# One reciprocal for the sums of a row's first two tiles, and GpSimd's weighing of both moved into the second turn

## The chip, the cores and the metric

The kernel runs on one core of a Trainium2 chip. The metric is device time in microseconds (us): the time of one execution, as a median over runs. The core has five engines that work side by side and hand work over by semaphores: TensorE (PE, matrix products into PSUM), VectorE (DVE), ScalarE (ACT), GpSimd (POOL) and SyncE (SP, DMA issues here). Each engine works its own list of instructions strictly in order, so an instruction that waits holds up all that stand behind it on its engine.

## The reference, cut to what matters

The input is `x` of shape (8, 512, 128). Each of the 8 batch rows has 4 tiles of 128 tokens, 32 tiles in all.

```python
xn = layernorm(x)
s  = attention(xn)                     # windows, compressed blocks and selected tokens, gated, normalised
# product-key expert layer, for each token and each of 8 heads
sx, ix = top_k(sim[0], 16)             # sim: 8 heads x 2 sides x 32 keys
sy, iy = top_k(sim[1], 16)
scores, pk = top_k(sx[:, None] + sy[None, :], 16)
h = gelu(x . W_down[pk]) * softmax(scores)
f = sum(h * W_up[pk])
out = x + s * silu(f)
```

The change touches only the `softmax(scores)`: its denominators are sums over the candidates of a head, inverted and multiplied onto the exponentials.

## The kernel before, in words

Only 50 of the 256 rank pairs of a head can be among its 16 best, so the kernel keeps 8 heads x 50 candidates for each token and finds which are in. A tile n passes these stations, spread over several turns of the loop:

- PE `scores(n)` writes the similarities into `sim_bank[n % 2]`. DVE `first_8` (16 MAX8), `strike_8` (pairs of MATCH_VALUE_LOAD and MATCH_REPLACE8) and `next_8` (16 MAX8) find the 16 best on each side.
- PE `top_columns` transposes them, ACT `take_topT` copies, PE `pair_gaps` makes the candidates' gaps in `t_bank`, ACT `take_gaps` copies them to `gap`. DVE `gaps_of_pairs`, `gaps_of_thirds` and `last_gaps` find a bound, `last8`.
- POOL `past_of`, ACT `side_of`, PE `transpose_sides`, ACT `take_sides`, POOL `square_of`, PE `count_places`, ACT `out_by_of`, POOL `drop_of` turn the bound into what each candidate loses.
- ACT `exps(n)` takes the exponentials into `prob[n % 2]` and, by its accumulator, their 8 sums into `den` (lines 797 to 810).
- DVE `invert_sums(n)` inverts the 8 sums (line 1104, `rden`). POOL `weigh(n)` multiplies (line 499, `wgt`), `add_halves(n)` and `add_quarters(n)` add heads (lines 505 and 512, `wgt4`, `wgt2`). PE `expert_weights(n)` transposes the result into `c_bank` (line 1504). Four tiles on, ACT `weights_out` copies the bank, POOL `gelu_times_weights` multiplies with the GELU values, PE `experts_out` makes the output, ACT `silu_parts` and POOL `gate_silu` gate it (lines 524, 853 to 856, 579).

Each engine has a hand-written function `turn(n)` for n = 4 to 31. With b, j = divmod(n, 4), b is the batch row and j = 0 to 3 the place in it, called here the first to the fourth turn of a row. In a turn n DVE finds the best of tile n, makes the bound of tile n - 1, and inverts the sums of tile n - 4, right behind `first_8(n)`. POOL makes `past` of tile n - 2, `drop` of n - 3, and weighs n - 4. The attention of row b - 1 or b is laid around it, differently in each of the four turns: `maxima` and `inverse_row_sums` (DVE, first turn), `scale_probs` (POOL, first turn), `attention_scores` (PE, first turn), `attention_out` (PE, third turn, in two halves around `top_columns`), `norm2` (POOL, third turn).

Two waits set the place of the vector work. `strike_8(n, 3)` waits until the last MAX8 of `first_8(n)` has signalled (line 1123). `gaps_of_pairs` waits for ACT's `gap` (line 1139).

## Time and profile before

| | us |
|---|---|
| median of three runs | 292.26 |
| the three runs | 293.19, 292.26, 290.89 |
| the profiled execution's own time | 290.93 |
| its span, first to last instruction | 289.2 |
| DVE busy | 267.4 (92%) |
| PE busy | 239.5 (83%) |
| ACT busy | 238.5 (82%) |
| POOL busy | 228.7 (79%) |

Busy is time in which an engine executes. In a row of the trace, an idle time in brackets is how long the engine waited ahead of that instruction, and the arrow names whose result ended the wait. Turns 4 to 31 fill the stretch from 60.4 us to 265 us; what stands before loads and folds weights, what stands behind is the end of the last row.

### The profile page before, as it was taken

To read this page: it belongs to the slowest core of one execution; us is meant where nothing else is said; L and a number is where in the kernel's file an instruction comes from. 1 tells how busy PE (TensorE), PEld (TensorE's weight loads), DVE (VectorE), ACT (ScalarE), POOL (GpSimd) and SP (SyncE) were. 2 spreads that over 40 slices of the span, in tenths; PEclk is the share of its full clock that TensorE was granted. 3 is DMA by queue.
4 is the path that set the end of the run, shared out by engine and by line. 5 is a ranking of instruction groups with operands and counts; after the bars stand their busy time and mean duration, and the time that the engine had idled before them with its cause. 6 is when DMAs were issued, how large, how long until landed. Compare 5 with 4: busy or idle time off the path is not lost.

```text
span 289.2 us, 7870 instructions
## 1 busy us (share of the span) xinstructions
PE 239.5 (83%) x1504; PEld 169.7 (59%) x1504; DVE 267.4 (92%) x2574; ACT 238.5 (82%) x1073; POOL 228.7 (79%) x351
## 2 busy tenths in 40 slices
PE   0779897787999888988898889888988898888672
PEld 0624343564767665766576657665766576656562
DVE  6679999989989999999999999999999999998464
ACT  3338668579789999999999999999999989997843
POOL 8986710377668879997999799979997999798792
PEclk9999999799599999999999999999999999999998
DMA  8920000000000000100010001000100010001002
GB/s 174 271 66 1 3 1 0 0 1 2 2 0 3 2 2 1 39 3 1 1 37 3 3 1 37 5 0 2 37 2 2 1 39 5 1 1 37 3 0 73
DMA packets 11234, 6.27 MB, mean 22 GB/s; under 512 B 1457, under 2 KB 10674, under 8 KB 11186
## 3 DMA queue, kind: packets, MB, share of 16 engines
q1 hardware_dynamic: 9858, 5.12, 6.8%
q10 hardware_dynamic: 1328, 0.66, 1.1%
q14 instruction: 36, 0.29, 0.3%
q8 instruction: 12, 0.20, 0.3%
HBM read 3.67 MB, written 2.10 MB: 20 GB/s over the span
## 4 chain that ended last, share of the span: by engine, by line
DVE 73%; PE 10%; ACT 7%; issue 6%; DMA 2%; ACTq 1%; DVEq 0%
DVE rest L1125 26%; DVE top L1114 15%; DVE top L1134 14%; DVE last L1158 6%; DMA fwq_sb<-in_L_ffn_Wq 2%; DVE slot_gap L1143 2%; DVE sel_m L1177 2%; PE sim L1456 1%; PE sim L1419 1%; ACT prob L808 1%; DVE st L1049 1%; PE scratch L1540 1%; DVE sel_b L1180 1%; DVE sel_a L1180 1%; DVE slot_gap L1149 1%
## 5 line engine op out<-in xcount | busy, mean ns | idle before, releaser
L1125 DVE MATCH_REPLACE8 rest<-top,sim 128x32 f32<-128x32 f32 x512 | 85.9, 180 | 0.0
L1134 DVE MAX8 top<-rest 128x8 f32<-128x32 f32 x512 | 53.5, 177 | 0.7
L808 ACT ACTIVATE prob<-drop 128x50 f32<-128x50 f32 x232 | 53.4, 255 | 0.0
L1114 DVE MAX8 top<-sim 128x8 f32<-128x32 f32 x496 | 50.9, 178 | 2.6 <-PE sim L1456 2.6
L808 ACT ACTIVATION_READ_ACCUMULATOR prob<-drop 128x1 f32 x232 | 48.6, 213 | 0.0
L488 POOL TENSOR_TENSOR squareT<-sideT 100x512 bf16<-100x512 bf16 x31 | 32.2, 1039 | 15.9 <-ACT sideT L723 15.9
L1125 DVE MATCH_VALUE_LOAD rest<-top,sim 128x8 f32 x512 | 41.1, 80 | 0.4
L1456 PE MATMUL sim<-sim_w,xT_all 128*128 128x512 f32 x64 | 35.3, 634 | 0.8 <-ACT xT_all L757 0.8
L473 POOL TENSOR_TENSOR past<-gap,last 128x400 f32<-128x400 f32 x31 | 26.7, 861 | 11.5 <-DVE last L1158 11.3
L495 POOL TENSOR_TENSOR drop<-gap,out_by 128x400 f32<-128x400 f32 x31 | 32.0, 1031 | 2.9 <-ACT out_by L714 2.9
L1474 PE MATMUL t_bank<-gaps_of,topT 128*128 128x200 f32 x128 | 29.7, 354 | 1.6 <-ACT topT L728 1.5
L501 POOL TENSOR_TENSOR wgt<-prob,rden 128x400 f32<-128x400 f32 x30 | 25.6, 853 | 5.8 <-DVE rden L1104 5.8
L1158 DVE MAX8 last<-slot_gap 128x8 f32<-128x22 f32 x256 | 24.0, 166 | 0.4
L1474 PEld LDWEIGHTS t_bank<-gaps_of,topT 128*128 128x128 f32 x128 | 20.4, 189 | 4.9 <-ACT topT L728 2.5
L723 ACT ACTIVATE sideT<-f_bank 100x512 bf16<-100x512 f32 x31 | 18.9, 608 | 2.8 <-PE f_bank L1486 2.8
L1465 PE MATMUL t_bank<-ident,top 128*128 128x128 f32 x64 | 13.3, 290 | 8.0 <-DVE top L1134 6.7
L1500 PE MATMUL f_bank<-count_s,sideT 101*128 101x100 bf16 x124 | 15.4, 210 | 5.5 <-POOL squareT L488 3.4
L1500 PEld LDWEIGHTS f_bank<-count_s,sideT 101*128 101x128 bf16 x124 | 11.4, 99 | 14.1 <-issue 14.1
L509 POOL TENSOR_TENSOR wgt<-wgt 128x200 f32<-128x200 f32 x30 | 18.2, 607 | 1.2
L735 ACT ACTIVATE gap<-t_bank 128x400 f32<-128x400 f32 x32 | 16.2, 507 | 2.5 <-PE t_bank L1474 2.4
L707 ACT ACTIVATE side<-past 128x400 bf16<-128x400 f32 x32 | 17.1, 534 | 0.6
L714 ACT ACTIVATE out_by<-f_bank 128x400 f32<-128x400 f32 x31 | 15.6, 503 | 2.2 <-PE f_bank L1501 2.2
(278 smaller groups left out, 714.6 us busy)
## 6 DMA issues: line engine op xcount, KB each, us to landing
out<-y_sb SPq DMA_DIRECT2D x7, 256.0 KB, 2.3
x_sb<-in_L_attn_hidden_states SPq DMA_DIRECT2D x2, 256.0 KB, 4.0
fwq_sb<-in_L_ffn_Wq ACTq DMA_DIRECT2D x2, 256.0 KB, 6.0
x_sb<-in_L_attn_hidden_states SPq DMA_DIRECT2D x1, 512.0 KB, 5.6
wc_sb<-in_L_attn_Wc SPq DMA_DIRECT2D x1, 256.0 KB
out<-last_y SPq DMA_DIRECT2D x2, 128.0 KB, 1.8
wo_in<-in_L_attn_Wo SPq DMA_DIRECT2D x1, 192.0 KB
keys_sb<-in_L_ffn_keys ACTq DMA_DIRECT2D x1, 128.0 KB, 3.5
```

What stands on the lines that cost most here:

```text
L473: nc.gpsimd.tensor_tensor(past[:, :, :], gap[n % 4][:, :, :], last8[n % 2][:, :, 7:8].to_broadcast([P, HEADS, CANDS]), ALU.subtract).then_ ...
L488: nc.gpsimd.tensor_tensor(squareT[0:TWO, :], sideT[0:TWO, :], sideT[0:TWO, :], ALU.mult).then_inc(square_done, 1)
L495: nc.gpsimd.tensor_tensor(drop[:, :, :], gap[n % 4][:, :, :], out_by[:, :, :], ALU.add).then_inc(drop_done, 1)
L501: nc.gpsimd.tensor_tensor(w[:, :, :], prob[n % 2][:, :, :], rden[n % 2][:, :].unsqueeze(2).to_broadcast([P, HEADS, CANDS]), ALU.mult).then ...
L808: last = nc.scalar.activation(prob[d][:, h, :], drop[:, h, :], ACT.Exp, scale=-1.0, accum_out=den[d][:, h:h + 1])
L1114: last = nc.vector.max(top[d][:, v, 0:8], sim_bank[d][:, bass.ts(v, KEYS)])
L1125: last = nc.vector.match_replace(out=rest[:, v, :], in_to_replace=top[d][:, v, 0:8], in_values=sim_bank[d][:, bass.ts(v, KEYS)], imm_value ...
L1134: last = nc.vector.max(top[n % 2][:, v, 8:16], rest[:, v, :])
L1158: last = nc.vector.max(last8[n % 2][:, h, :], slot_gap[:, h, :])
L1456: mm(sim_bank[n % 2][:, :], xT_all[:, bass.ts(n, P)], sim_w[:, :], start=True, stop=True).then_inc(sim_ready, 1)
L1474: last = mm(t_bank[:, bass.ts(k, HALF_H * CANDS)], topT[:, bass.ts(k, P)], gaps_of[:, :, :].rearrange("p h c -> p (h c)"), start=True, sto ...
L1500: mm(o, sideT[0:TWO + 1, bass.ts(k, P)], count_s[0:TWO + 1, :], start=True, stop=False)
```

## The change

Four parts, all inside the turns:

1. `den` and `rden` become one tile each, with both parities side by side. DVE no longer inverts in the first turn of a row. In the second turn a new `invert_pair(n - 5)` inverts 16 sums by one operation, those of tiles n - 5 and n - 4.
2. POOL no longer weighs in the first turn. In the second turn it weighs tile n - 5 between `past_of` and `drop_of`, adds its halves and quarters, squares, and then weighs and adds tile n - 4.
3. PE leaves `expert_weights` out of the first turn; it does the row's first tile (n - 5) in the second turn and its second tile (again n - 5) in the third, between the halves of `attention_out`. The fourth turn stays.
4. In the third turn POOL does `past_of` ahead of `gate_silu`, where it did it behind.

```diff
 # POOL
                 if j == 0:
                     past_of(n - 2)
                     drop_of(n - 3)
-                    weigh(n - 4)
-                    add_halves(n - 4)
                     if b >= 2:
                         gelu_times_weights(b - 2)
-                    add_quarters(n - 4)
                     square_of(n - 2)
                     scale_probs(b - 1)
                 elif j == 1:
                     past_of(n - 2)
+                    weigh(n - 5)
                     drop_of(n - 3)
+                    add_halves(n - 5)
+                    add_quarters(n - 5)
+                    square_of(n - 2)
                     weigh(n - 4)
                     add_halves(n - 4)
                     add_quarters(n - 4)
-                    square_of(n - 2)
                 elif j == 2:
+                    past_of(n - 2)
                     if b >= 2:
                         gate_silu(b - 2)
-                    past_of(n - 2)
                     weigh(n - 4)
 # DVE
+            def invert_pair(n):
+
+                dve.wait_ge(prob_done, n + 2)
+                if n >= 1:
+                    dve.wait_ge(wgt_done, n)
+                nc.vector.reciprocal(rden[:, :, :], den[:, :, :]).then_inc(rden_done, 2)
...
                 if j == 0:
                     first_8(n)
-                    invert_sums(n - 4)
                     strike_8(n, 3)
...
                 elif j == 1:
                     first_8(n)
-                    invert_sums(n - 4)
+                    invert_pair(n - 5)
                     strike_8(n, 3)
 # PE
                     values_out(b - 1)
-                    expert_weights(n - 4)
                     block_values_out(b - 1)
                     count_places(n - 2)
...
                     project_window(b, U_KW, wk_sb)
-                    expert_weights(n - 4)
+                    expert_weights(n - 5)
                     count_places(n - 2)
                 elif j == 2:
                     attention_out(b - 1, range(2))
+                    expert_weights(n - 5)
                     top_columns(n - 1)
```

The third turn of PE keeps its own `expert_weights(n - 4)` later on. The rows that follow are instructions in program order, with their line and, behind the tile names, the shape; line numbers after the change are shifted by a few.

On DVE, in the first turn of the fourth row (tile 16 is found, tile 12's sums inverted), before:

```order
L1114 MAX top<-sim 128x8 x16
L1104 RECIPROCAL rden<-den 128x8
L1125 MATCH_REPLACE rest<-top,sim 128x32 x4
L1208 TENSOR_REDUCE nmax<-s_bank 128x4
L1210 TENSOR_REDUCE nmax<-s_bank 128x1
```

and after, at the same place:

```order
L1120 MAX top<-sim 128x8 x16
L1131 MATCH_REPLACE rest<-top,sim 128x32 x4
L1214 TENSOR_REDUCE nmax<-s_bank 128x4
L1216 TENSOR_REDUCE nmax<-s_bank 128x1
L1218 TENSOR_REDUCE nmax<-s_bank 64x1
```

The reciprocal is gone from between MAX8 and MATCH_REPLACE8; in the second turn the same place has one of 128x16 where it had one of 128x8.

On POOL, the second turn of a row and the start of the third (`wgt_0` and `wgt_1` are the quarters' sums of an even and an odd tile), before:

```order
L473 TENSOR_TENSOR past<-gap,last_1 128x400
L495 TENSOR_TENSOR drop<-gap,out_by 128x400
L501 TENSOR_TENSOR wgt<-prob,rden 128x400
L509 TENSOR_TENSOR wgt<-wgt 128x200
L516 TENSOR_TENSOR wgt_1<-wgt 128x100
L488 TENSOR_TENSOR squareT<-sideT 100x512
L579 TENSOR_TENSOR y<-tanh_f,half_f 128x512
L473 TENSOR_TENSOR past<-gap,last_0 128x400
L501 TENSOR_TENSOR wgt<-prob,rden 128x400
```

and after:

```order
L472 TENSOR_TENSOR past<-gap,last_1 128x400
L500 TENSOR_TENSOR wgt<-prob,rden 128x400
L494 TENSOR_TENSOR drop<-gap,out_by 128x400
L508 TENSOR_TENSOR wgt<-wgt 128x200
L515 TENSOR_TENSOR wgt_0<-wgt 128x100
L487 TENSOR_TENSOR squareT<-sideT 100x512
L500 TENSOR_TENSOR wgt<-prob,rden 128x400
L508 TENSOR_TENSOR wgt<-wgt 128x200
L515 TENSOR_TENSOR wgt_1<-wgt 128x100
L472 TENSOR_TENSOR past<-gap,last_0 128x400
L578 TENSOR_TENSOR y<-tanh_f,half_f 128x512
L500 TENSOR_TENSOR wgt<-prob,rden 128x400
```

Three operations more stand ahead of the third turn's `past`, and `drop` stands behind a weighing where it stood ahead of it.

On PE, in the third turn, around the halves of `attention_out`, before:

```order
L1626 MATMUL s_bank<-off_mean,xT_all 128x128
L1628 MATMUL s_bank<-vwc,pT_cs 128x128
L1629 MATMUL s_bank<-vwc,pT_cs 128x128
L1630 MATMUL s_bank<-vww,pT_win 128x128
L1626 MATMUL s_bank<-off_mean,xT_all 128x128
L1630 MATMUL s_bank<-vww,pT_win 128x128
L1465 MATMUL t_bank<-ident,top 128x128 x2
```

and after:

```order
L1631 MATMUL s_bank<-off_mean,xT_all 128x128
L1633 MATMUL s_bank<-vwc,pT_cs 128x128
L1634 MATMUL s_bank<-vwc,pT_cs 128x128
L1635 MATMUL s_bank<-vww,pT_win 128x128
L1631 MATMUL s_bank<-off_mean,xT_all 128x128
L1635 MATMUL s_bank<-vww,pT_win 128x128
L1521 MATMUL c_bank<-ident,wgt_1 100x128
L1470 MATMUL t_bank<-ident,top 128x128 x2
```

One transposition of weights has come in ahead of `top_columns`; the one that left stood in the first turn, between `values_out` and `block_values_out`.

## Rows read from the trace of the kernel before

**Rows 1.** Busy time by engine in the steady turns (us, instructions, clock, DMA)

```profile
core 0: us, PE busy (x) PEld busy (x) DVE busy (x) ACT busy (x) POOL busy (x), PEclk, DMA share, GB/s
84.50:264.00 179.50, 159.04 (x1068) 117.83 (x1067) 178.81 (x1894) 168.99 (x807) 161.24 (x217) 1.00 0.03 9
```

**Rows 2.** Waits of DVE over the span (us in total, times, longest us)

```profile
DVE slot_gap L1143 <- ACT gap L735: 1.7, 2, 1.1
```

**Rows 3.** Timeline of DVE, second and third turn (start us, us, operation)

```profile
128.46 1.65 DVE L1114 MAX8 top<-sim 128x8 f32<-128x32 f32 x16
130.03 0.18 DVE L1104 RECIPROCAL rden<-den 128x8 f32<-128x8 f32 x1
130.21 0.09 DVE L1125 MATCH_VALUE_LOAD rest<-top,sim 128x8 f32 x1
...
136.97 0.18 DVE L1104 RECIPROCAL rden<-den 128x8 f32<-128x8 f32 x1
```

**Rows 4.** Timeline of DVE, tile 2, where no reciprocal stands between

```profile
33.66 1.65 DVE L1114 MAX8 top<-sim 128x8 f32<-128x32 f32 x16
35.41 0.09 DVE L1125 MATCH_VALUE_LOAD rest<-top,sim 128x8 f32 x1
```

**Rows 5.** Groups of instructions by form: reciprocals on DVE (busy us, mean ns)

```profile
L1104 DVE RECIPROCAL rden<-den 128x8 f32<-128x8 f32 x32 | 5.8, 182 | 0.7 <-ACT prob L808 0.6
...
L1198 DVE RECIPROCAL gnorm<-gsum 128x32 f32<-128x32 f32 x1 | 0.4, 352 | 0.1
```

**Rows 6.** Timeline of POOL, second turn's end, third, and the next first

```profile
132.75 1.04 POOL L488 TENSOR_TENSOR squareT<-sideT 100x512 bf16<-100x512 bf16 x1
134.46 1.26 POOL L579 TENSOR_TENSOR y<-tanh_f,half_f 128x512 f32<-128x512 f32 x1 [0.68 <-ACT tanh_f L856]
135.69 0.86 POOL L473 TENSOR_TENSOR past<-gap,last 128x400 f32<-128x400 f32 x1
137.22 0.85 POOL L501 TENSOR_TENSOR wgt<-prob,rden 128x400 f32<-128x400 f32 x1 [0.67 <-DVE rden L1104]
138.04 1.03 POOL L495 TENSOR_TENSOR drop<-gap,out_by 128x400 f32<-128x400 f32 x1
139.03 0.60 POOL L509 TENSOR_TENSOR wgt<-wgt 128x200 f32<-128x200 f32 x1
...
140.06 1.04 POOL L488 TENSOR_TENSOR squareT<-sideT 100x512 bf16<-100x512 bf16 x1
...
142.73 0.86 POOL L473 TENSOR_TENSOR past<-gap,last 128x400 f32<-128x400 f32 x1 [0.36 <-DVE last L1158]
...
156.11 0.20 POOL L553 TENSOR_TENSOR rgate<-rinv,gates 128x4 f32<-128x4 f32 x1 [0.45 <-DVE rinv L1203]
```

**Rows 7.** Timeline of PE, third turn's end to the next first

```profile
141.25 0.20 PE L1500 MATMUL f_bank<-count_s,sideT 101*128 101x100 bf16 x1 [0.31 <-POOL squareT L488]
...
142.00 0.41 PE L1465 MATMUL t_bank<-ident,top 128*128 128x128 f32 x2 [0.22 <-DVE slot_gap L1149]
...
149.91 0.30 PE L1579 MATMUL s_bank<-win_mask,ident 128*128 128x320 bf16 x1
...
151.25 0.33 PE L1587 MATMUL s_bank<-kcs,qcs 128*64 128x64 f32 x2
```

**Rows 8.** Timeline of ACT, fourth turn

```profile
144.34 0.50 ACT L735 ACTIVATE gap<-t_bank 128x400 f32<-128x400 f32 x1 [0.18 <-PE t_bank L1474]
...
149.13 0.41 ACT L820 ACTIVATE kcs<-scratch,bk_sb 128x192 f32<-128x192 f32 x1
```

**Rows 9.** Timeline of DVE, fourth turn and next first

```profile
145.65 0.33 DVE L1143 TENSOR_TENSOR slot_gap<-t_bank,gap 128x176 f32<-128x176 f32 x1
...
151.92 0.48 DVE L1208 TENSOR_REDUCE nmax<-s_bank 128x4 f32<-128x320 f32 x1
```

**Rows 10.** Busy time by engine in three stretches, columns as in rows 1

```profile
67.90:71.30 3.40, 1.79 (x14) 1.31 (x12) 3.40 (x37) 3.40 (x23) 2.90 (x7) 1.00 0.02 5
71.30:78.20 6.90, 6.54 (x27) 4.27 (x25) 6.90 (x75) 5.72 (x27) 4.26 (x6) 0.51 0.01 2
153.40:156.80 3.40, 2.40 (x22) 1.72 (x20) 3.37 (x36) 3.40 (x23) 2.87 (x6) 1.00 0.00 0
```

More of the change, by code:

```diff
@@ L228, in program @@
         drop = sb("drop", [P, HEADS, CANDS])
-        den = [sb(f"den{i}", [P, HEADS]) for i in range(2)]
-        rden = [sb(f"rden{i}", [P, HEADS]) for i in range(2)]
+        den, rden = sb("den", [P, 2, HEADS]), sb("rden", [P, 2, HEADS])
         prob = [sb(f"prob{i}", [P, HEADS, CANDS]) for i in range(2)]
@@ L501, in weigh @@
                 nc.gpsimd.tensor_tensor(w[:, :, :], prob[n % 2][:, :, :],
-                                        rden[n % 2][:, :].unsqueeze(2).to_broadcast([P, HEADS, CANDS]),
+                                        rden[:, n % 2, :].unsqueeze(2).to_broadcast([P, HEADS, CANDS]),
                                         ALU.mult).then_inc(wgt_done, 1)
@@ L808, in exps @@
                     last = nc.scalar.activation(prob[d][:, h, :], drop[:, h, :], ACT.Exp, scale=-1.0,
-                                                accum_out=den[d][:, h:h + 1])
+                                                accum_out=den[:, d, h:h + 1])
                 last.then_inc(prob_done, 1)
@@ L1099, in invert_sums @@
                         dve.wait_ge(rden_done, n - 1)
-                    nc.vector.tensor_reduce(den[d][:, :], prob[d][:, :, :], AX_X, ALU.add).then_inc(sum_done, 1)
+                    nc.vector.tensor_reduce(den[:, d, :], prob[d][:, :, :], AX_X, ALU.add).then_inc(sum_done, 1)
                     dve.wait_ge(sum_done, sums_until(n))
@@ L1103, in invert_sums @@
                     dve.wait_ge(wgt_done, n - 1)
-                nc.vector.reciprocal(rden[d][:, :], den[d][:, :]).then_inc(rden_done, 1)
+                nc.vector.reciprocal(rden[:, d, :], den[:, d, :]).then_inc(rden_done, 1)
+            def invert_pair(n):
[3 more added lines that the diff above has]
+                nc.vector.reciprocal(rden[:, :, :], den[:, :, :]).then_inc(rden_done, 2)
             def first_8(n):
@@ L1350, in last_weigh @@
                 nc.vector.tensor_tensor(wgt[m % 2][:, :, :], prob[m % 2][:, :, :],
-                                        rden[m % 2][:, :].unsqueeze(2).to_broadcast([P, HEADS, CANDS]),
+                                        rden[:, m % 2, :].unsqueeze(2).to_broadcast([P, HEADS, CANDS]),
                                         ALU.mult).then_inc(last_wgt, 1)
```

## The prediction

> **What bounds the kernel now.** I read first the busy time by engine over the steady turns [rows 1]: in 179.5 us DVE is busy for 178.81, the other four for at most 169. Then I read DVE's waits: asked for the same stretch the view lists none, and the last one ahead of it is the longer of the two for ACT's `gap`, 1.1 us in the third turn of row 1 [rows 2]. So from the fourth turn of row 1 on the time is the sum of what DVE issues, and a change gains only what it takes from DVE's issue. It loses as soon as one of the results that DVE reads comes later than DVE does. Both have to be worked out.
>
> **The edits on DVE.** Seven reciprocals go (first turns of rows 1 to 7) and seven grow from 8 to 16 elements. By duration alone that would be 7 x 0.18 = 1.3 us saved. But the timeline shows what stands around one [rows 3]. The 16 MAX8 begin at 128.46 and end at 130.11. The reciprocal starts at 130.03, under the last MAX8's end, and the next operation starts at 130.21, 0.10 after that end. For tile 2 no reciprocal stands in this place [rows 4]: the MAX8 end at 33.66 + 1.65 = 35.31 and the next operation starts at 35.41, again 0.10 later. The cover is the wait of `strike_8` for the signal of the last MAX8. The reciprocal lies inside this gap, and taking it away leaves the gap. I take 0 per removed reciprocal; the bound on the gaining side is its whole 0.18.
>
> The grown one: 8 elements take 182 ns and 32 take 352 [rows 5], so (352 - 182) / 24 = 7 ns an element, and 16 take 0.24 us. In the row above, 0.18 us of it just reach the next start at 130.21; 0.06 more may show, or not, since DVE overlaps operations (the reciprocal itself starts 0.08 before the MAX8 end). I take 0, with 7 x 0.06 = 0.4 us as the losing bound.
>
> The Trainium skill, page "VectorE: DVE Perf Modes", section "The TRN2 errata", gives a VectorE operation from SBUF a fixed 58 cycles plus one cycle an element, at 0.96 GHz. By it a merge would save 61 ns, seven of them 0.4 us; the trace disagrees with the slope (7 ns an element, not 1) and, above all, the gap of 0.10 us stays without the operation.
>
> **The edits on POOL.** They remove nothing, they move 0.85 + 0.60 + 0.4 us from the first turn of each row into the second. I follow one row of the batch, in the times of before.
> - Second turn. `weigh` of the first tile now stands behind `past` and has to wait for the pair's reciprocal: 130.03 + 0.24 = 130.27 [rows 3], and about 0.07 more, the step from the reciprocal's end at 137.15 to `weigh` at 137.22 in the next turn [rows 3, 6]: 130.34. From there the steps of the third turn [rows 6]: `weigh` to `drop` 0.82, `drop` to halves 0.99, halves to `square` 1.03, so `square` starts at 133.18 where it started at 132.75: 0.43 late. Behind it come `square` (1.01), the second `weigh` with the wait for its own result (0.92) and halves and quarters (1.03): the third turn's `past` starts at 136.14, for 135.69: 0.45 late.
> - Third turn. The 0.68 us that POOL idled ahead of `y` are used up. `past` 0.82, `y` 1.24, so `weigh` starts at 138.20 for 137.22: 0.98 late, and with it `drop`, halves, and `square` at 141.04 for 140.06.
> - Fourth turn. `past` had waited 0.36, so it is 0.98 - 0.36 = 0.62 late. No other idle time follows up to the first turn, where the 1.85 us are gone: POOL arrives early at the last waiting place there, `rgate` at 156.11, and all delay ends. The work is the same and POOL does not become the bound.
>
> **Who waits for these.** PE's `count_places` in the third turn waits for `square`: 141.25 becomes 142.23. Behind it in PE's order stands `top_columns` of the next tile. It started at 142.00 after a wait of 0.22 for DVE [rows 7], so it could have started at 141.78; now 141.78 + 0.98 = 142.76, 0.76 late. The chain goes on through ACT's `topT` and PE's `pair_gaps` to ACT's `gap`, which waited for PE [rows 8]: 144.34 becomes 145.10, and ends at 145.60. DVE reads it at 145.65 [rows 9]. The slack was 0.81 and becomes 0.05, no more than a signal takes. I count 0.
>
> ACT stays 0.76 late to the end of that turn, since it had followed PE there: `kcs` ends at 149.54 + 0.76 = 150.30 [rows 8]. PE's `attention_scores` waits for it, with about 0.07 for the signal: 150.37 for 149.91, 0.46 late. Its last product ends at 151.58 + 0.46 = 152.04, with the signal 152.10 [rows 7]; DVE wants it at 151.92 for `maxima` [rows 9]. That is a wait of 0.18 us in the first turn of rows 3 to 7, five times: 0.9 us. What is late next, ACT's exponentials of the windows, is behind DVE anyway. Rows 1 and 2 have less work on POOL (no `y` in row 1), there I count nothing for it. PE's one transposition more in row 1's third turn and a late start of the tail I price together at 0.1.
>
> **Sum.** 0 (removed) + 0 (grown) + 0.9 + 0.1 = +1.0 us on the profiled execution of 290.93. Its time stands 1.3 below the median of the three, 292.26, which I take as the base: **293.3 us**.
>
> **The rivals.**
> - *The reciprocals count after all and no wait appears.* For it: a wait of 0.18 is the difference of a chain of six steps, each good to 0.1, and DVE's delay anywhere relieves all others. Against it: rows 3 and 4. It gives 292.3 - 1.3 to 292.3: about 291.6.
> - *A bigger loss by the same chain* (the other side). Place: `gap` in the fourth turn and `maxima` in the first. It decides from a chain later than 0.75 us, where both begin to wait together. If each step adds 0.5 us more (`top_columns` held by the new transposition ahead of it in the third turn, `row_squares` behind the late `attention_out`), DVE loses 0.6 in each of 6 rows: +3.6, 295.9.
> - *TensorE's clock falls in each row.* In row 1 PE was busy for 1.79 of 3.4 us, and then the granted clock was 0.51 of full, the lower of its two levels of 1.2 and 2.4 GHz, up to 78.2 us; the `gap` of 1.1 us came after that [rows 2, 10]. In later first turns PE is busy for 2.40 of 3.4 at full clock, and the change makes that less: `count_places` no longer waits for POOL, so PE waits longer for DVE behind it. It decides if PE's idle time nearly doubles; I reckon 0.6 more at most, which leaves 1.8 of 3.4, just there. Price: 1.1 us in each of 6 rows, +6.6, 298.9. The Trainium skill's page "TensorE: Matmul & The Clock Gate", Part 1, says the same in words: throttled is the default, and activity releases it.
> - *A gain above 1%.* DVE would have to issue 2.9 us less, and its seven reciprocals are 1.3. Only a measurement would show this.
>
> **How the numbers follow.** Forecast (a loss of 0 to 2.5): 0.56, own range 292.3 to 294.8. No wait, or a small gain: 0.26. Bigger loss by the chain: 0.10. Clock: 0.05. Gain above 1%: 0.03. The 1%, 2.9 us, is about what a measurement of this kernel can tell from no change. Slower by over 1% (above 295.2) holds most of the chain's and clock's cases, 0.13; faster 0.05; the rest 0.82. The range reaches from the small gain with all seven reciprocals, 291.0, to the chain at two thirds of its price and some of the spread of the runs, 295.4; outside are the clock, the chain at its full price and the large gain, under 2 in 10.
>
> **What would show it.** Right: the start of the operation behind the MAX8 in a first turn 0.10 us behind their end, with no reciprocal there; the pair at about 0.24 us; POOL's third-turn `square` about 1 us later against DVE's MAX8 of its turn; short waits of DVE for `nmax`, about 0.2 us each, five times, and DVE busy for some 99% of the turns. Wrong: the gap shrinks to nothing in the first turn (then the reciprocal did cost); waits at `slot_gap` in each fourth turn (the chain is longer); a granted clock of half in the first turns (the clock); no wait at all and a period of a row as before (the slack is larger than worked out).

## The result and the profile after

| | before | after |
|---|---|---|
| median, us | 291.51 | 293.25 |
| lowest to highest, us | 288.93 to 293.19 | 290.74 to 295.56 |
| runs | 20 | 20 |
| profiled execution, us | 290.93 | 293.73 |
| its span, us | 289.2 | 292.0 |

The ratio of the changed kernel to the one before is 1.0074, with a 95% interval of 1.0048 to 1.010; the two medians alone would give 1.0060. That is a loss of 0.6 to 0.7%, and 293.25 stands beside the forecast of 293.3. The mechanism behind the forecast is another matter.

The page of the profile after, its span, its busy times and the granted clock of TensorE in 40 slices:

```profile
span 292.0 us, 7858 instructions
PE 237.9 (81%) x1504; PEld 170.6 (58%) x1504; DVE 267.3 (92%) x2567; ACT 238.4 (82%) x1073; POOL 228.7 (78%) x351
PEclk9999999998999999999999979997999899999997
```

DVE is busy for 267.3 us, where it was for 267.4, although seven reciprocals are gone. So the 2.8 us that the span grew by are idle time of DVE. The waits of DVE over the whole span (us in total, times, longest us) name where the forecast had looked and where it had not:

```profile
DVE slot_gap L1149 <- ACT gap L734: 4.2, 4, 1.3
...
DVE nmax L1214 <- PE s_bank L1592: 0.7, 2, 0.5
```

The forecast wanted about five more waits of 0.2 us for `nmax`. That row held 1.7 us in 2 waits before and holds 0.7 in 2 now, of which the longer, at 63.35, is row 1's. The other, 0.17 us, stands at 241.2, and the timeline has two of 0.07 at 180.4 and 210.8; all three come in the first turn behind a long wait for `gap`. Instead `slot_gap` waits 4.2 us, where it waited 1.7 [rows 2].

**Account by rows.** The start of the large `nmax` reduction in each first turn marks the rows: row 1 reaches from the one at 64.12 us before (63.35 after) to the next. The steps between them, in us, are:

| row | before | after |
|---|---|---|
| 1 | 30.07 | 28.90 |
| 2 | 28.87 | 28.88 |
| 3 | 28.86 | 28.88 |
| 4 | 28.87 | 30.40 |
| 5 | 28.87 | 30.43 |
| 6 | 28.86 | 30.39 |
| 7 | 28.57 | 28.59 |

Rows 2 and 3 take the same time as before to 0.02 us: in them the change is free. Rows 4 to 6 lose 1.53, 1.56 and 1.53, together 4.62 us. Row 1 gains 1.17, the head ahead of it 0.77, row 7 loses 0.02, the end 0.07: 4.62 + 0.03 + 0.02 + 0.07 - 1.17 - 0.77 = 2.8, which is the difference of the spans.

**What happens in row 4.** Here are two stretches of row 3's and row 4's third turns that end the same way, then the 3.4 us behind the latter; then the stretch of the kernel before that answers to the first. The two and the last one end 0.30 to 0.35 us behind the start of `count_places` (columns as in rows 1). After:

```profile
137.20:140.60 3.40, 1.68 (x12) 0.68 (x11) 3.33 (x35) 3.39 (x20) 3.24 (x6) 1.00 0.00 0
166.10:169.50 3.40, 1.69 (x13) 0.71 (x12) 3.33 (x35) 3.37 (x20) 3.24 (x6) 1.00 0.00 0
169.50:172.90 3.40, 3.40 (x18) 2.74 (x15) 3.18 (x35) 1.48 (x4) 3.40 (x4) 0.50 0.02 5
```

Before:

```profile
138.20:141.60 3.40, 2.63 (x17) 1.41 (x16) 3.37 (x38) 3.40 (x24) 3.24 (x6) 1.00 0.00 0
```

PE's busy time up to there fell from 2.63 us to 1.68, in every row from row 2 on. (In the kernel before PE then waited 0.22 us more for DVE; the 3.4 us up to `top_columns` itself, from 138.53, hold 2.49.) In rows 4 to 6 the granted clock then was 0.50 of full for 3.4 us, which is the lower of TensorE's two levels, 1.2 GHz in place of 2.4. In row 3 it stayed at full. The rows of PE show what the lost busy time is, and what the clock does to the work behind it. After, row 4 (x is the count, brackets are the idle time ahead):

```profile
165.66 1.02 PE L1461 MATMUL sim<-sim_w,xT_all 128*128 128x512 f32 x2
168.08 0.32 PE L1521 MATMUL c_bank<-ident,wgt 128*100 128x128 f32 x1 [1.40 <-POOL wgt L515]
168.23 0.62 PE L1545 MATMUL scratch<-xT_all,wv_sb 128*128 128x272 f32 x2
169.17 0.20 PE L1505 MATMUL f_bank<-count_s,sideT 101*128 101x100 bf16 x1 [0.31 <-POOL squareT L487]
...
169.56 0.65 PE L1470 MATMUL t_bank<-ident,top 128*128 128x128 f32 x2
...
172.04 1.36 PE L1479 MATMUL t_bank<-gaps_of,topT 128*128 128x200 f32 x4
```

PE waits 1.40 us for POOL's quarters and 0.31 for its `square`. The second wait stood there before too [rows 7]. The first was 0.45 us before; after, it is as long in all six rows from row 2 on. First the row of the kernel before, then the waits of the changed one between 84.5 and 266.8 us:

```profile
140.16 0.32 PE L1516 MATMUL c_bank<-ident,wgt 128*100 128x128 f32 x1 [0.45 <-POOL wgt L516]
```

```profile
PE c_bank L1521 <- POOL wgt L515: 8.4, 6, 1.4
```

In the half-clock stretch of row 4 `top_columns` takes 0.65 us where it takes 0.40 at full clock (140.67 us, below), and `pair_gaps` 1.36 for 0.94. ACT waits for both, and DVE for ACT:

```profile
170.25 0.38 ACT L727 ACTIVATE topT<-t_bank 128x256 f32<-128x256 f32 x1 [0.78 <-PE t_bank L1470]
172.15 0.27 ACT L817 ACTIVATE xsel<-scratch 64x128 f32<-64x128 f32 x1 [1.12 <-PE scratch L1559]
173.43 0.50 ACT L734 ACTIVATE gap<-t_bank 128x400 f32<-128x400 f32 x1 [0.59 <-PE t_bank L1479]
...
173.97 0.34 DVE L1149 TENSOR_TENSOR slot_gap<-t_bank,gap 128x176 f32<-128x176 f32 x1 [1.29 <-ACT gap L734]
```

`gap` ends at 173.93 and DVE starts at 173.97, after 1.29 us of waiting. Waits of 1.29 at 204.40 and 0.92 at 234.70 are the same thing in rows 5 and 6. The fourth of the four, 0.68, is in the tail at 271.3.

Row 6 has one thing more: DVE stands idle for 0.16 us at 232.53, where the profile names nothing that it waits for. The same idle time stands in row 6 of every profile of a kernel that has `invert_pair` (this one and four of those below) and in none of the others. Where no wait for `gap` comes behind it in that row, row 6 takes 0.25 us more than its neighbours. Its cause is open.

**Where the clock does not fall**, the steps of the forecast can be held against row 3 of after. Subtract 1.91 from the times of the forecast, since `nmax` begins at 150.01 for 151.92. Rows of PE, ACT and DVE in order of time:

```profile
140.67 0.40 PE L1470 MATMUL t_bank<-ident,top 128*128 128x128 f32 x2
...
143.00 0.50 ACT L734 ACTIVATE gap<-t_bank 128x400 f32<-128x400 f32 x1 [0.17 <-PE t_bank L1479]
...
143.73 0.33 DVE L1149 TENSOR_TENSOR slot_gap<-t_bank,gap 128x176 f32<-128x176 f32 x1
...
147.58 1.65 DVE L1120 MAX8 top<-sim 128x8 f32<-128x32 f32 x16
...
147.79 0.41 ACT L819 ACTIVATE kcs<-scratch,bk_sb 128x192 f32<-128x192 f32 x1
...
149.34 0.09 DVE L1131 MATCH_VALUE_LOAD rest<-top,sim 128x8 f32 x1
...
149.60 0.33 PE L1592 MATMUL s_bank<-kcs,qcs 128*64 128x64 f32 x2
...
150.01 0.48 DVE L1214 TENSOR_REDUCE nmax<-s_bank 128x4 f32<-128x320 f32 x1
```

### The profile page after: what moved, and what is told of

It is laid out like the page before. It is cut to its first block, busy times and chain, and to the rows that moved or that the text cites. A ratio compares the mean times of both kernels' runs of the same rounds, so it can differ in the third digit from the quotient of the medians.

```text
span 292.0 us, 7858 instructions
## 1 busy us (share of the span) xinstructions
PE 237.9 (81%) x1504; PEld 170.6 (58%) x1504; DVE 267.3 (92%) x2567; ACT 238.4 (82%) x1073; POOL 228.7 (78%) x351
## 4 chain that ended last, share of the span: by engine, by line
DVE 56%; PE 14%; POOL 11%; issue 9%; ACT 6%; DMA 2%; SPq 1%; DVEq 0%; ACTq 0%; POOLq 0%
DVE rest L1131 19%; DVE top L1140 10%; DVE top L1120 9%; DVE last L1164 4%; POOL wgt L500 3%; ACT prob L807 3%; PE scratch L1552 3%; PE scratch L1559 2%; POOL squareT L487 2%; DMA x_sb<-in_L_attn_hidden_states 2%; POOL wgt L508 2%; PE t_bank L1479 2%; POOL past L472 2%; DVE sel_m L1183 2%; DVE st L1048 2%
## 5 line engine op out<-in xcount | busy, mean ns | idle before, releaser
L1479 PE MATMUL t_bank<-gaps_of,topT 128*128 128x200 f32 x128 | 31.3, 370 | 1.5 <-ACT topT L727 1.5
L1479 PEld LDWEIGHTS t_bank<-gaps_of,topT 128*128 128x128 f32 x128 | 21.9, 202 | 5.3 <-issue 2.5
```

The source lines that it names most:

```text
L1479: last = mm(t_bank[:, bass.ts(k, HALF_H * CANDS)], topT[:, bass.ts(k, P)], gaps_of[:, :, :].rearrange("p h c -> p (h c)"), start=True, sto ...
```

## The experiments

Each ratio is against runs of the kernel before on the same chip, with its 95% interval; like the one above it can differ from the quotient of the two medians. A statement on rows is from one profiled execution each. Theory A says that the loss is TensorE's clock, which falls behind PE's longer idle time in the third turn. Its rivals are that the later results themselves make DVE wait, or that the reciprocals count.

**The changed kernel once more.** No edit.

> The changed kernel itself, on the same chip and beside the same runs of the kernel before as the next three. Expected 0.5 to 1% above the kernel before, with TensorE waiting 1.4 us for the quarter sums in each third turn, and stretches at half clock after some of them. If it comes out within 0.3% of the kernel before here, the difference hangs on where the clock happens to fall, and not on the order alone.

Measured: 293.87 us, ratio 1.0115 (1.0081 to 1.015). The slices of TensorE's clock:

```profile
PEclk9999999998999999999999999999999799979857
```

Rows 1 to 5 take 28.86 to 28.89 us, row 6 takes 30.41 and row 7 30.02 where it took 28.57 before. The clock fell in other rows than above, and again for 10.2 us in the tail. The stretch ahead of one fall, and the fall:

```profile
223.70:227.10 3.40, 1.69 (x11) 0.64 (x10) 3.33 (x34) 3.40 (x21) 3.24 (x6) 1.00 0.00 0
227.20:230.60 3.40, 3.40 (x17) 2.74 (x15) 3.24 (x34) 1.48 (x4) 3.40 (x4) 0.51 0.03 7
```

PE was again busy for 1.69 of 3.4 us. The idle pattern is in every row from row 2 on, the fall follows it in some and not in others, and which ones differs between executions. So the loss is a frequency times about 1.5 us, and one profile doesn't give the median.

**More work for PE in the third turn of the changed kernel.** The product of `scores(n + 1)` is issued twice (the new second argument), which fills the idle time with 0.85 us.

```diff
                     pair_gaps(n - 1)
-                    scores(n + 1)
+                    scores(n + 1, 2)
                     expert_weights(n - 4)
```

> The changed kernel with the product of scores(n + 1) issued twice in the third turn of every row (same operands, same result, some 0.9 us more of TensorE work), laid into TensorE's wait of 1.40 us for GpSimd's quarter sums. Theory A (the loss is TensorE's clock, which falls after this idle time): no stretch at half clock from the third turns, DVE's waits of 0.9 to 1.3 us for gap in the fourth turns are gone, and the time comes down by 1.5 to 2.5 us against the changed kernel, to within 0.3% of the kernel before. Theory B (the chain over square, top_columns and gap is simply too long, at whatever clock): the extra work doesn't help; DVE's waits for gap stay, and the time stays 0.7% above the kernel before or more.

Measured: 291.11 us, ratio 1.0028 (0.9996 to 1.006). The stretch at the end of the third turn:

```profile
137.90:141.30 3.40, 2.53 (x14) 1.07 (x13) 3.33 (x35) 3.38 (x20) 3.24 (x6) 1.00 0.01 2
```

and PE's waits for the quarters:

```profile
PE c_bank L1523 <- POOL wgt L515: 3.3, 6, 0.6
```

The wait for the quarters shrank from 1.4 us to 0.6, since PE now executes in it; POOL is as late as in the changed kernel. Half clock is left only at 54 and 71 us and at the end. Rows 1 to 5 take 28.88 to 28.90 us, row 6 with its idle 0.16 us takes 29.12, and no wait for `gap` is left in the steady turns. Useless work took the loss out of the rows: it is the idleness of PE, not the lateness of POOL's results.

**The same in the kernel before.** It is the control: does the second product help by itself?

```diff
                     pair_gaps(n - 1)
-                    scores(n + 1)
+                    scores(n + 1, 2)
                     expert_weights(n - 4)
```

> Control: the kernel before with the same second product of scores(n + 1) in the third turn. There TensorE waited 0.45 us for the quarter sums, so 0.4 us of the extra 0.9 delay what stands behind. Theory A: the clock did not fall in its turns from row 2 on, so there is nothing to win there; the same time within 0.3%, at most a little slower. Rival (more TensorE work is good for this kernel anywhere, since its clock falls in row 1 and in some executions elsewhere): 0.3 to 1% faster.

Measured: 290.99 us, ratio 1.0011 (0.9984 to 1.0038). It does not, so the gain in the changed kernel is not a gain of the product itself.

**`gate_silu` behind `square_of` in the third turn of the changed kernel.** It was to have the quarters and `square` ready some 1.2 us earlier, without work for PE.

```diff
                     past_of(n - 2)
-                    if b >= 2:
-                        gate_silu(b - 2)
                     weigh(n - 4)
...
                     square_of(n - 2)
+                    if b >= 2:
+                        gate_silu(b - 2)
```

> The changed kernel with one more move on GpSimd: in the third turn gate_silu (1.26 us) goes behind square_of, so weigh, drop, halves, quarters and square come up to 1.2 us earlier. Theory A (TensorE idles for GpSimd's quarter sums, then its clock falls): TensorE's wait for the quarter sums shrinks from 1.40 us to below 0.5, the half clock in third and fourth turns is gone, and the time is within 0.3% of the kernel before. Theory B (the loss comes from the second turn, where drop stands behind a weighing and square is 0.43 us late): nothing changes there, the time stays 0.5 to 1% above the kernel before.

Measured: 290.94 us, ratio 1.0016 (0.999 to 1.0042). The quarters come 1.0 us earlier, since POOL now waits 0.22 us for the third turn's reciprocal. The same stretch, PE's waits, and the clock in 40 slices:

```profile
136.20:139.60 3.40, 2.88 (x20) 1.66 (x18) 3.37 (x37) 3.40 (x23) 3.32 (x5) 1.00 0.00 0
```

```profile
PE c_bank L1521 <- POOL wgt L515: 2.2, 7, 0.4
```

```profile
PEclk9999999998999999999999999999999999999997
```

No fall is left between 74 us and the end. Rows 1 to 5 take 28.88 to 28.90 us, row 6 29.13. Two opposite ways of taking PE's idle time away, more work and earlier inputs, take the same loss away.

**Two reciprocals again, the rest of the change kept.** If the merge itself were free, this would be as slow as the changed kernel.

```diff
 # first turn
                     first_8(n)
+                    invert_sums(n - 4)
                     strike_8(n, 3)
 # second turn
                     first_8(n)
-                    invert_pair(n - 5)
+                    invert_sums(n - 4)
                     strike_8(n, 3)
```

> The changed kernel with two reciprocals of 8 sums as before, one in the first and one in the second turn, in place of one of 16; GpSimd's and TensorE's orders stay changed. Theory A (a reciprocal lies inside the 0.10 us that DVE waits for its own MAX8's signal): the same time as the changed kernel within 0.2%, with the next operation of DVE 0.10 us behind the end of the MAX8 in both turns. Rival (each reciprocal costs DVE its 0.18 us): 1.3 us slower than the changed kernel, less 0.4 for the shorter operations, so some 0.3% slower than it.

Measured: 291.01 us, ratio 1.001 (0.998 to 1.004), and rows 1 to 6 of 28.88 to 28.93 us. The expectation was missed: the kernel is about as fast as before. The reason is on POOL, in the second turn. First this kernel, then the changed one:

```profile
128.32 0.86 POOL L472 TENSOR_TENSOR past<-gap,last 128x400 f32<-128x400 f32 x1
129.14 0.85 POOL L500 TENSOR_TENSOR wgt<-prob,rden 128x400 f32<-128x400 f32 x1
```

```profile
155.91 0.86 POOL L472 TENSOR_TENSOR past<-gap,last 128x400 f32<-128x400 f32 x1
157.29 0.86 POOL L500 TENSOR_TENSOR wgt<-prob,rden 128x400 f32<-128x400 f32 x1 [0.52 <-DVE rden L1110]
```

With a reciprocal of its own, a turn old, the first tile's `weigh` starts right behind `past`. With the pair's it waits 0.52 us. All that POOL does up to the end of the third turn shifts by about this. In the third turn, as a row of PE's timeline and as the stretch around it:

```profile
140.05 0.32 PE L1522 MATMUL c_bank<-ident,wgt 128*100 128x128 f32 x1 [0.96 <-POOL wgt L515]
```

```profile
138.00:141.40 3.40, 2.13 (x13) 0.90 (x12) 3.33 (x35) 3.40 (x23) 3.24 (x6) 1.00 0.00 0
```

PE waits 0.96 us for 1.40, is busy for 2.13 for 1.68, and the clock does not fall behind any third turn. So the "one operation for two" of the change, which frees DVE of nothing, costs PE 0.45 us of work in this stretch, and this decides.

**Both at once:** two reciprocals and `gate_silu` behind `square_of`, the edits of two kernels above together.

```diff
                     past_of(n - 2)
-                    if b >= 2:
-                        gate_silu(b - 2)
                     weigh(n - 4)
...
                     square_of(n - 2)
+                    if b >= 2:
+                        gate_silu(b - 2)
 # first turn
                     first_8(n)
+                    invert_sums(n - 4)
 # second turn
                     first_8(n)
-                    invert_pair(n - 5)
+                    invert_sums(n - 4)
```

> The changed kernel with both mends: a reciprocal of 8 sums in the first and one in the second turn, and gate_silu behind square_of in the third turn. TensorE's wait for the quarter sums should be 0.2 us or less; rows of 28.9 us without half-clock stretches; the time within 0.2% of the kernel before, since DVE has as much to do. It can beat it only if the clock falls less often than there.

Measured: 290.86 us, ratio 1.0007 (0.998 to 1.0033). DVE has no wait at all between 84.5 and 262 us; rows 1 to 6 take 28.87 to 28.89 us. PE's wait ahead of the third turn's transposition:

```profile
138.29 0.32 PE L1522 MATMUL c_bank<-ident,wgt 128*100 128x128 f32 x1 [0.24 <-POOL wgt L515]
```

It is shorter than the 0.45 of the kernel before, and nothing comes of it, because PE's wait was no cost there. This is the best variant of the change, and it equals the kernel before.

**The fourth part undone: `gate_silu` ahead of `past_of` again, in the changed kernel.**

```diff
                 elif j == 2:
-                    past_of(n - 2)
                     if b >= 2:
                         gate_silu(b - 2)
+                    past_of(n - 2)
                     weigh(n - 4)
```

> The changed kernel with its fourth part undone: in the third turn gate_silu stands ahead of past_of again. weigh and square keep their times, past is 1.2 us later than in the changed kernel. By the chain (ACT's side_of waits for past and holds up row_squares, sideT and gap behind it) gap of the third turn ends about 1.2 us later, where it had 0.5 us of slack: DVE waits for it some 0.7 us in each third turn of rows 2 to 7, 3 to 4 us more than the changed kernel, 1.5 to 2.5% above the kernel before. Rival (ACT has slack there): as the changed kernel.

Measured: 292.82 us, ratio 1.0076 (1.0043 to 1.011). Here the later results do reach DVE. ACT waits for `past`, and DVE for `gap` in the third turn of each row (a timeline row of ACT, a row of DVE's waits between 84.5 and 264 us):

```profile
138.06 0.54 ACT L706 ACTIVATE side<-past 128x400 bf16<-128x400 f32 x1 [1.11 <-POOL past L472]
```

```profile
DVE slot_gap L1149 <- ACT gap L734: 1.6, 6, 0.3
```

Rows 2 to 5 take 29.24 us, 0.36 over the 28.88, about half of what was expected; row 6, with its idle 0.16 us, takes 29.49, and row 7 28.94 for 28.57. The clock does not fall in them: POOL's quarters are as late against DVE as in the changed kernel, but PE, itself held up, waits for them only 0.20 us and is busy for 2.9 of the 3.4 us ahead of `top_columns`. So part 4 of the change is needed, and without it a loss of the forecast's kind comes, DVE waiting for a late result at full clock. With and without part 4 the time is about the same, for different reasons.

**POOL late in the kernel before.** An extra POOL product of 128x400, into a tile that nobody reads, was to make the quarters late without the change. It is placed ahead of `weigh`:

```diff
                     past_of(n - 2)
+                    xs = x_sb[:, 0:TB, :].rearrange("p t d -> p (t d)")[:, 0:HEADS * CANDS]
+                    nc.gpsimd.tensor_tensor(idle_tile[:, :], xs, xs, ALU.mult)
                     weigh(n - 4)
```

> The kernel before with one extra GpSimd product of 128x400 (1.03 us, into a tile that nobody reads) in the third turn, between past_of and weigh. It makes the third turn's quarter sums and square about 1 us late, as the change did, and changes nothing else. Theory A (this lateness is the whole cost, by way of TensorE's idle time and its clock): TensorE's wait for the quarter sums goes from 0.45 to 1.4 us, half-clock stretches appear after third turns, each with a wait of DVE for gap of 0.9 to 1.3 us in the fourth turn, and the time is 0.5 to 1% above the kernel before. Rival (the second turn's order, or the weights moved on TensorE, cost the time): no difference to the kernel before.

Measured: 289.66 us, ratio 0.9983 (0.9954 to 1.0011). The product took 0.85 us and vanished in the 0.67 that POOL waits there for the reciprocal [rows 6]; PE's wait grew only to 0.55, and the expected loss did not come. The test did not make the condition that it was to test, and says nothing on A.

**The same one place later,** behind `weigh`:

```diff
                     weigh(n - 4)
+                    xs = x_sb[:, 0:TB, :].rearrange("p t d -> p (t d)")[:, 0:HEADS * CANDS]
+                    nc.gpsimd.tensor_tensor(idle_tile[:, :], xs, xs, ALU.mult)
                     drop_of(n - 3)
```

> The kernel before with one extra GpSimd product of 128x400 (1.03 us, into a tile that nobody reads) in the third turn, now behind weigh, where GpSimd has no wait left in which it could hide. Theory A (lateness of the quarter sums, TensorE's idle time, TensorE's clock): TensorE's wait for the quarter sums goes from 0.45 to 1.4 us, half-clock stretches follow some third turns, rows with one take 1.5 us more, rows without one take 28.87 us, and the time is 0.7 to 1.2% above the kernel before, like the changed kernel. Rival (the changed kernel loses by its other moves): the same time as the kernel before.

Measured: 291.12 us, ratio 1.0022 (0.9996 to 1.0047). PE now waits 1.26 us. Two stretches at a third turn's end, and the one behind the second; then DVE's wait:

```profile
138.00:141.40 3.40, 1.83 (x12) 0.67 (x11) 3.33 (x35) 3.35 (x20) 3.24 (x6) 1.00 0.01 2
225.00:228.40 3.40, 1.82 (x15) 0.92 (x14) 3.37 (x37) 2.92 (x19) 3.24 (x6) 1.00 0.00 0
228.40:231.80 3.40, 3.40 (x13) 2.72 (x12) 2.96 (x32) 1.47 (x4) 3.40 (x5) 0.50 0.03 7
```

```profile
DVE slot_gap L1146 <- ACT gap L738: 1.2, 1, 1.2
```

The clock fell once in six rows, that row took 30.30 us and the others 28.85 to 28.90. The mechanism is thus made in the kernel before, by lateness alone; the size, expected at 0.7 to 1.2%, was missed, and the median is not clear of the kernel before. Behind 1.82 us of work the clock fell in one row of six, behind 1.69 in three and in two of six; what decides in a single row these runs do not show.

**Row 1 filled in the kernel before.** Four products of 128x128 behind the first turn's `count_places`, in row 1 only, where the clock fell before [rows 10]:

```diff
                     count_places(n - 2)
+                    if b == 1:
+                        for _ in range(4):
+                            mm(c_bank[:, 3 * P:4 * P], ident[:, :], ident[:, :], start=True, stop=True)
```

> The kernel before with four extra TensorE products of 128x128 (into the free quarter of c_bank) behind count_places in row 1's first turn, where TensorE was idle 0.94 us and then 0.67 us, ahead of the stretch at half clock. If the clock can be kept up by work in idle time, no half-clock stretch follows at 71 us, the wait of 1.1 us for gap in row 1's third turn is gone, and the median is 0.3 to 0.8 us below the kernel before. Rival (that fall has its cause elsewhere): the same time within 0.2%.

Measured: 290.75 us, ratio 1.0018 (0.9989 to 1.0046). In its profile the row 1 fall and the `gap` wait are gone and row 1 takes 28.88 us for 30.07, but the median did not move, where 0.3 to 0.8 us less were expected. Nor can the profile credit the fill: three others that leave row 1 as it was (the control above, the first late product of POOL, and the reciprocals left out, below) show no fall in row 1 either, and 28.88 to 28.90 us. In this execution the clock was half for 10.2 us in the tail, at 272. What a profile shows gained in one row need not be in the median.

**The first turn's reciprocals left out of the kernel before.** Rows 2 to 7 use older inverses, so part of the softmax is left out.

```diff
                     first_8(n)
-                    invert_sums(n - 4)
+                    if b == 1:
+                        invert_sums(n - 4)
+                    else:
+                        dve.wait_ge(prob_done, n - 3)
+                        dve.sem_inc(rden_done, 1)
                     strike_8(n, 3)
```

> The kernel before without the reciprocal of the first turn in rows 2 to 7, and nothing in its place (GpSimd weighs the first tile of those rows by the inverses of an earlier tile; that part of the softmax is left out). Theory A (the reciprocal lies inside DVE's 0.10 us wait for its own MAX8): the operation behind the MAX8 starts 0.10 us after their end as before, a row takes 28.87 us as before, the time is the same within 0.2%. Rival (a reciprocal costs 0.18 us of DVE): a row takes 28.7 us, the time is 1.1 us (0.4%) lower.

Measured: 291.44 us, ratio 1.0032 (1.0004 to 1.0059), rows 1 to 6 of 28.85 to 28.88 us, unchanged. DVE's timeline:

```profile
147.57 1.64 DVE L1114 MAX8 top<-sim 128x8 f32<-128x32 f32 x16
149.32 0.09 DVE L1125 MATCH_VALUE_LOAD rest<-top,sim 128x8 f32 x1
```

149.32 - (147.57 + 1.64) = 0.11, against 0.10 with the reciprocal: the gap and the rows are as expected. The median is not: 0.3% more, where the same within 0.2% was expected. Of this rows 1 to 6 hold nothing. Row 7 takes 28.89 us for 28.57, with DVE idle for 0.31 us at 251.03 behind nothing that the profile names, and in the tail the clock was half for 10.2 us.

**A second reciprocal behind each in the kernel before,** of 128x8 of a constant:

```diff
                 nc.vector.reciprocal(rden[d][:, :], den[d][:, :]).then_inc(rden_done, 1)
+                if not summed(n):
+                    nc.vector.reciprocal(spare8[:, :], neg_half[:, 0:HEADS])
```

> The kernel before with one more reciprocal of 128x8 (of a constant, into a tile that nobody reads) behind each of the 29 of the turns. Theory A (the first one is hidden in 0.10 us of waiting, which it fills up): the second one shows in full or nearly, 0.10 us each by the distance at which DVE starts its operations: rows of 29.3 us, the time 2.5 to 3 us (1%) higher. Rival 1 (reciprocals are hidden anyhow): the same time. Rival 2 (each costs 0.18): rows of 29.6 us, 5 us higher.

Measured: 291.48 us, ratio 1.005 (1.0022 to 1.0079). DVE's timeline:

```profile
127.12 1.65 DVE L1117 MAX8 top<-sim 128x8 f32<-128x32 f32 x16
128.69 0.18 DVE L1105 RECIPROCAL rden<-den 128x8 f32<-128x8 f32 x1
128.79 0.15 DVE L1107 RECIPROCAL spare<-neg_half 128x8 f32<-128x8 f32 x1
128.87 0.09 DVE L1128 MATCH_VALUE_LOAD rest<-top,sim 128x8 f32 x1
```

The next operation starts 0.10 us behind the MAX8's end with two reciprocals between as with one: the rival, hidden anyhow, was right. Three rows take 29.00 to 29.02 us and three 28.86 to 28.88, so some 0.4 us of the 0.5% are in the rows, for a reason that the profile does not name. Where the rest is I have not settled; in the tail the clock was half for 10.2 us here too.

**The granted clock of all executions.** A profile is one execution, but the mean granted clock and the time are on record for each. The last column is the mean time less that of the kernel before beside it, in us:

| kernel | executions | mean granted clock | mean time |
|---|---|---|---|
| before, beside the experiments | 103 | 0.983 | |
| changed, first measurement | 20 | 0.973 | +1.96 |
| changed, once more | 12 | 0.972 | +3.10 |
| changed, PE's third turn filled | 12 | 0.982 | +0.73 |
| changed, `gate_silu` late | 12 | 0.985 | +0.30 |
| changed, two reciprocals | 12 | 0.985 | +0.24 |
| changed, both | 12 | 0.983 | +0.33 |
| changed, fourth part undone | 10 | 0.984 | +2.26 |
| before, PE's third turn filled | 12 | 0.980 | +0.29 |
| before, POOL late ahead of `weigh` | 12 | 0.985 | -0.61 |
| before, POOL late behind `weigh` | 12 | 0.978 | +0.73 |
| before, row 1 filled | 12 | 0.979 | +0.40 |
| before, first reciprocals left out | 12 | 0.977 | +1.01 |
| before, second reciprocals | 12 | 0.976 | +1.09 |

The changed kernel stands lowest. The four variants of it that give PE more work in that stretch are at the level of the kernel before, and so is the one whose loss is DVE's wait at full clock. An estimate: a stretch of 3.4 us at half takes 3.4 x 0.5 / 292 = 0.0058 off the mean. The changed kernel's second measurement and the runs beside it differ by 0.0111 (0.9827 and 0.9716), which is 1.9 such stretches in an execution, at 1.5 us each 2.9 us, for 3.10 measured. The mean doesn't say where the clock was low: the last three of the table have low means too, and their profiles show it in the tail (10.2 us in each) and not in the rows.

## Why the prediction was right or wrong

**Right: what bounds the kernel, and that the edits on DVE are worth nothing.** In rows 2 and 3 of after a row takes 28.88 us, for 28.87 and 28.86 before. The gap behind the MAX8 is 149.34 - 149.23 = 0.11 without a reciprocal, and with the pair's (157.16 - 157.06) it is 0.10:

```profile
155.41 1.65 DVE L1120 MAX8 top<-sim 128x8 f32<-128x32 f32 x16
156.97 0.24 DVE L1110 RECIPROCAL rden<-den 128x16 f32<-128x16 f32 x1
157.16 0.09 DVE L1131 MATCH_VALUE_LOAD rest<-top,sim 128x8 f32 x1
```

The pair took the 0.24 us of the estimate, of which none shows. Leaving the reciprocal out and doubling it gave the same gap. The rival by which the reciprocals count is refuted. (The 61 ns that the forecast works out from the Trainium skill should read 60, which changes nothing.)

**Right: how late POOL becomes.** In row 3's third turn `weigh` starts at 136.28, which is 138.19 in the forecast's times (forecast 138.20), and PE's wait for `square` ends at 140.30, or 142.21 (forecast 142.23).

**Wrong in size: the chain to DVE, by one step.** The forecast put `top_columns` 0.53 us behind the start of `count_places` (141.78 - 141.25) and so 0.76 late. It stands 140.67 - 140.30 = 0.37 behind. Its start at 142.00 had been set by a wait for DVE, and how much earlier PE could have begun was read off the length of that wait; it was 0.16 more. So it is 0.58 late (140.67 + 1.91 - 142.00), and every later step carries this: `gap` ends at 143.50 with 0.23 us of slack ahead of DVE's 143.73 (forecast 0.05), `kcs` starts 0.57 late (147.79 + 1.91 - 149.13), and the last product of `attention_scores` ends at 149.93, 0.26 late (forecast 0.46), ahead of DVE's 150.01. **The term that failed is the "wait of 0.18 us in the first turn of rows 3 to 7, five times: 0.9 us".** It is 0 in the rows at full clock, which is the forecast's own last sign of being wrong: no wait and a period as before. A wait worked out as the difference of two chains was as large as the error of one of its steps, and the forecast's first rival had said so.

**Wrong in place: the clock.** The forecast named TensorE's clock as a rival with 0.05, but looked for it in the first turn only, where PE loses its wait for POOL. In its own list of those who wait stood the sentence that failed: "PE's `count_places` in the third turn waits for `square`: 141.25 becomes 142.23". The 0.98 us were passed on to ACT and DVE as lateness and never counted as idle time of PE. With them the third turn's 2.63 busy of 3.4 us would have been 1.65, just under the 1.79 of row 1 that the clock had fallen behind [rows 10]. What was measured is 1.68. The waits at `slot_gap` in the fourth turn, which the forecast would have read as a longer chain, came from the clock. Each fall costs 1.5 us, in three rows of six in one profile and in two in the other; the forecast's price of 1.1 in each of six rows was too small per fall and too high in number. The Trainium skill's page "TensorE: Matmul & The Clock Gate", Part 1, says that throttled is the default and activity releases the clock; by it a lateness that leaves PE without work can be a cost of its own, and here the trace agrees in three rows of six: granted clock 0.50 behind 1.67 to 1.69 us of work in 3.4.

**So the total was right for a wrong reason.** The forecast had +1.0 us, from +0.9 by waits that did not come. It was added to a base of 292.26, the median of three runs, which the 20 runs put at 291.51. So the base was 0.75 too high and the loss 0.74 too low, and that 293.3 met 293.25 is luck. The measured +1.74 (293.25 - 291.51) is the clock: shown by rows 2 and 3 of the profile, as late and at full clock without loss, by two ways of taking PE's idle time away, which bring the ratio to 1.0028 and 1.0016, and by the two that put it there (the change, and once in six rows the late POOL in the kernel before). The head and row 1, which gained 1.9 us in the profile of after, also are matters of the clock and vary between executions. They hide part of the 4.6 us, and the forecast had not a word on them. The small medians left over, 0.1 to 0.5%, are as large as what the head and the tail give or take in the profiles (the tail of the run without first reciprocals is 1.8 us longer than before); 0.25 us of them are row 6 where `invert_pair` is kept, and for the rest no cause is given.

## What to carry to other kernels

When a feeder of TensorE becomes later, add its lateness to TensorE's idle time of that stretch, besides following the results on, and hold the busy time that is left against stretches in the trace behind which the granted clock fell. An operation that lies in an engine's wait for its own result is free, so merging it with another gains nothing, while whoever reads the merged result may have to wait for the later of two inputs; look for who reads the earlier half. A wait computed as the difference of two chains is only as good as their worst step, and a profile's total should be split by row and by its head and tail before the median is explained.

## What the runs showed of the hardware that was not expected

- The same idle pattern (PE busy 1.67 to 1.69 us of 3.4, waits of 1.40 and 0.31) was followed by half clock in three rows of six in one execution and in two in another. Of the other third turns, one in six fell behind 1.82, none behind 2.04 and more, and none behind 1.95 to 1.97, which row 1 has in four of the profiles.
- In the third turns a fall lasted 3.4 us and cost DVE 1.5 us a row, because the half-clock stretch lies on `top_columns` and `pair_gaps`, with 0.23 us of slack behind them. In row 1 it lasted 6.8 us before and 3.4 after, where row 1 took 28.90 us: there it cost nothing.
- Behind a group of 16 MAX8, DVE's next dependent operation starts 0.10 to 0.11 us after their end, with nothing, one reciprocal of 8 or of 16 elements, or two reciprocals of 8 between them.
- DVE stood idle for 0.16 us at the same operation of row 6 in all five profiles of kernels with one reciprocal for two tiles, and in none of the nine others.
